# Layer 2 of a four-layer graph network: the boundary between row groups one quad sooner, and products and low parts interleaved

## The reference

```python
h = jnp.maximum(_layernorm(x, axis=-1), 0.0)
x = x + _L2_gnn_ref(h, adj, L2_gnn_W, L2_gnn_a)

def _L2_gnn_ref(x, adj, W, a):
    h = x @ W
    e_src = h @ a[:D, 0]
    e_dst = h @ a[D:, 0]
    e = e_src[:, None] + e_dst[None, :]
    e = jnp.where(e > 0, e, NEG_SLOPE * e)
    att_logits = jnp.where(adj > 0, e, MASK_VAL)
    attention = jax.nn.softmax(att_logits, axis=1)
    h_prime = attention @ h
    return jax.nn.elu(h_prime)
```

## Time and profile before

| | us |
|---|---|
| median of 3 runs | 2366.55 |
| lowest, highest | 2362.13, 2367.09 |
| the profiled execution | 2364.97 |
| its span in the trace | 2363.3 |
| mean granted clock of TensorE | 0.983 |

### The profile page before, as it was taken

How to read it: one execution, slowest core, us unless ns; L and a number is a source line. 1 busy time by engine, 2 the same in 40 slices (tenths; PEclk the granted TensorE clock), 3 DMA queues, 4 the chain that set the end, 5 groups by cost and what they waited for, 6 DMA issues and landing times. The chain is left out here.

```text
span 2363.3 us, 45615 instructions
## 1 busy us (share of the span) xinstructions
PE 2228.8 (94%) x17180; PEld 1702.6 (72%) x17180; DVE 1799.8 (76%) x2845; ACT 1372.6 (58%) x2100; POOL 114.6 (5%) x124
## 2 busy tenths in 40 slices
PE   5799999999999998999978999999999999999998
PEld 4677767778676776888867888878466666666667
DVE  6967788697877856112249999998898898898896
ACT  6555564655656465665655555554465565565656
POOL 2000010010101001000000000000000000000000
PEclk9899999999999999999989999999999999999999
DMA  7542240414321012222211222222211111111000
GB/s 177 112 63 42 58 85 28 81 45 81 51 62 50 28 52 96 81 89 93 80 45 50 71 69 70 67 75 68 84 32 47 31 54 50 36 46 50 23 32 28
DMA packets 62934, 146.72 MB, mean 62 GB/s; under 512 B 10023, under 2 KB 14778, under 8 KB 61757
## 3 DMA queue, kind: packets, MB, share of 16 engines
q1 hardware_dynamic: 56461, 110.57, 15.1%
q0 software_dynamic: 5760, 33.56, 8.6%
q10 hardware_dynamic: 560, 0.52, 0.1%
HBM read 170.30 MB, written 41.43 MB: 90 GB/s over the span
## 5 line engine op out<-in xcount | busy, mean ns | idle before, releaser
L2150 PE MATMUL bank<-VB,arena 128*128 128x257 f16 x1024 | 285.7, 279 | 30.6 <-ACT arena L2036 21.8
L193 PE MATMUL bank<-s_row,kT_hi 128*128 128x512 f16 x1024 | 304.5, 379 | 3.4 <-DVE m_col L2743 1.2
L1559 PE MATMUL bank<-VA,ph 128*128 128x257 f16 x1024 | 281.3, 275 | 6.8 <-DVE VA L1168 6.8
L2153 PE MATMUL bank<-VB,arena 128*128 128x257 f16 x1024 | 284.5, 278 | 0.0
L2151 PE MATMUL bank<-VB,arena 128*128 128x257 f16 x1024 | 284.4, 278 | 0.0
L2857 PE MATMUL bank<-VA,w_dense 128*128 128x257 f16 x1024 | 280.7, 274 | 3.0 <-ACT w_dense L2681 2.4
L1560 PE MATMUL bank<-VA,ph 128*128 128x257 f16 x1024 | 280.9, 274 | 0.0
L1561 PE MATMUL bank<-VA,pl 128*128 128x257 f16 x1024 | 280.8, 274 | 0.0
L2859 PE MATMUL bank<-VA,arena 128*128 128x257 f16 x1024 | 280.2, 274 | 0.0
L2858 PE MATMUL bank<-VA,w_dense 128*128 128x257 f16 x1024 | 280.1, 274 | 0.0
L2015 ACT CAST arena<-arena 128x512 f16<-128x512 f32 x256 | 155.8, 617 | 157.8 <-DVE arena L2067 139.5
(11 more groups left out here) (344 smaller groups left out, 4937.7 us busy)
## 6 DMA issues: line engine op xcount, KB each, us to landing
mask<-mask_d SPq DMA_DIRECT2D x128, 256.0 KB, 2.7
arena<-mask_d SPq DMA_DIRECT2D x128, 256.0 KB, 2.7
mask_d<-in_adj POOLq DMA_DIRECT2D x8, 2048.0 KB, 23.4
xg<-in_x SPq DMA_DIRECT2D x8, 512.0 KB, 11.9
x<-xg SPq DMA_DIRECT2D x8, 512.0 KB, 3.9
xg<-x SPq DMA_DIRECT2D x8, 512.0 KB, 4.2
x<-xo POOLq DMA_DIRECT2D x8, 512.0 KB, 3.0
w_dense<-x SPq DMA_DIRECT2D x8, 512.0 KB, 4.2
```

Source lines behind the costliest of these rows:

```text
L193: last = nc.tensor.matmul(out_ap, st, mv, start=(i == 0), stop=(i == len(todo) - 1))
L1559: nc.tensor.matmul(acc, ph[:, u % HR, c], v_row(V, 0, t), start=(t == 0), stop=False)
L2150: nc.tensor.matmul(acc, p_hi, v_at(V, 0, t), start=first, stop=False)
L2153: last = nc.tensor.matmul(acc, pl[:, slot(q, r), c], v_at(V, 0, t), start=False, stop=final)
```

## The change

Four things. `late` is 0 in layer 2 too, so the reciprocals and scalings stand in part 0 instead of part 1, the fourth reciprocal in quad 1, and the parts with the elu, the moments, the normalisation, the transposes and the split of kT each stand one quad sooner; the queries and values (TensorE's q = 5, the splits' q = 7) stay. Relu and Exp stay in part 1, and so now stand behind the high parts of quad 1, apart from the scalings. Within a quad VectorE takes products and low parts in the order of `ORDER`, with nb ahead of low part 0. After the loop `beside` is called once with -1 ahead of the parts, and its steps are numbered one lower, which leaves that end in its old sequence. The waits that named a product or a low part by number now name it by its place in the new order; they are left out of the diff.

```diff
@@ -1919,7 +1919,7 @@
                 ring = 4 if weighted else 2
-                late = 1 if weighted else 0
+                late = 0 if weighted else 0
                 ph = tile("ph", [P, ring * R, GW], F16)
@@ -1939,7 +1939,8 @@
                 act_q.plan(("hi", R))
-                dve_q.plan(("p32", R), ("lo", R))
+                ORDER = [("p32", 0), ("p32", 1), ("lo", 0), ("p32", 2), ("lo", 1), ("p32", 3), ("lo", 2), ("lo", 3)]
+                dve_q.plan(*((f"{name}{r}", 1) for name, r in ORDER))
                 skip = 0 if weighted else Q - 1
@@ -1970,6 +1971,8 @@
                             part(eng, g - 1, q)
+                    if beside is not None:
+                        beside(-1)
                     for q in range(Q):
...
@@ -2029,7 +2032,7 @@
                     def part(act, g, q):
-                        if q == late:
+                        if q == 0:
                             work["sums_free"](act, g)
@@ -2060,21 +2063,22 @@
                             dve.wait_ge(gam_rowed.sem, gam_rowed.upto(q))
-                        for r in range(R):
-                            dve.wait_ge(dve_q.sem, dve_q.before(n, "lo", r))
-                            if r == 2 and q == 1 + late and not isinstance(g, int):
-                                inverse(g - 1, R - 1, R)
-                            nc.vector.scalar_tensor_tensor(
-                                out=p32[:, r, :], in0=s_row[:, ds(g * GW, GW)],
-                                scalar=omega[:, q * R + r:q * R + r + 1],
-                                in1=mask[:, q % MS, r * GW:(r + 1) * GW], op0=ALU.max, op1=ALU.mult
-                                ).then_inc(dve_q.sem, dve_q.one("p32", r))
-                        if not isinstance(g, int):
-                            middle(g - 1, q)
-                        for r in range(R):
-                            dve.wait_ge(act_q.sem, act_q.at(n, "hi", r))
-                            nc.vector.tensor_tensor(pl[:, slot(q, r), :], p32[:, r, :], ph[:, slot(q, r), :],
-                                                    ALU.subtract).then_inc(dve_q.sem, dve_q.one("lo", r))
+                        for name, r in ORDER:
+                            if name == "p32":
+                                if r == 1 and q == 1 and not isinstance(g, int):
+                                    inverse(g - 1, R - 1, R)
+                                dve.wait_ge(dve_q.sem, dve_q.before(n, f"lo{r}"))
+                                nc.vector.scalar_tensor_tensor(
+                                    out=p32[:, r, :], in0=s_row[:, ds(g * GW, GW)],
+                                    scalar=omega[:, q * R + r:q * R + r + 1],
+                                    in1=mask[:, q % MS, r * GW:(r + 1) * GW], op0=ALU.max, op1=ALU.mult
+                                    ).then_inc(dve_q.sem, dve_q.one(f"p32{r}"))
+                            else:
+                                if r == 0 and not isinstance(g, int):
+                                    middle(g - 1, q)
+                                dve.wait_ge(act_q.sem, act_q.at(n, "hi", r))
+                                nc.vector.tensor_tensor(pl[:, slot(q, r), :], p32[:, r, :], ph[:, slot(q, r), :],
+                                                        ALU.subtract).then_inc(dve_q.sem, dve_q.one(f"lo{r}"))
                         if isinstance(g, int):
@@ -2451,12 +2455,11 @@
                     nc.scalar.activation(e[:, :], ag[:, :], ACT.Relu, scale=-1.0).then_inc(act_s.sem, act_s.one("below"))
-                if q == 1:
                     act.wait_ge(act_s.sem, act_s.at(g, "below"))
                     nc.scalar.activation(e[:, :], e[:, :], ACT.Exp, scale=-1.0).then_inc(act_s.sem, act_s.one("e"))
-                if q == 3:
+                if q == 2:
                     normal(act, g, h, xo, nb, rsx)
-                if q == 5:
+                if q == 4:
                     act.wait_ge(pe_s.sem, pe_s.at(g, "hT", K - 1))
@@ -2467,11 +2470,11 @@
             def dve_middle(dve, g, q):
-                if q == 3:
+                if q == 2:
                     shift(dve, g, nb, mvx, rsx, "nb", "rx")
...
             def dve_part(dve, g, q):
-                if q == 2:
+                if q == 1:
@@ -2681,11 +2684,11 @@
                 def beside(q):
-                    if q == 0:
+                    if q < 0:
                         far_pair(0)
                         far_pair(1)
-                    if 2 <= q <= 5:
-                        far_pair(q)
+                    if 1 <= q <= 4:
+                        far_pair(q + 1)
@@ -2781,17 +2784,17 @@
                 def beside(q):
-                    if q == 0:
+                    if q < 0:
                         own_entries(0)
+                    if q == 1:
+                        add_far(1)
                     if q == 2:
-                        add_far(1)
-                    if q == 3:
                         take_top(1)
...
                         take_top(2)
+                    if q == 3:
+                        add_far(3)
                     if q == 4:
-                        add_far(3)
-                    if q == 5:
                         take_top(3)
```

More of the change, by code:

```diff
@@ L1980, in quad @@
                     def quad(g, q):
-                        eng, stage = (dve_q, "p32") if weighted else (act_q, "hi")
-                        sp.wait_ge(eng.sem, eng.before(g * Q + q, stage, R - 1, MS))
+                        sp.wait_ge(*((dve_q.sem, dve_q.before(g * Q + q, "p323", 0, MS)) if weighted else
+                                     (act_q.sem, act_q.before(g * Q + q, "hi", R - 1, MS))))
                         sp.sem_inc(s_pass[3], 1)
@@ L2011, in quad @@
                             if weighted:
-                                act.wait_ge(dve_q.sem, dve_q.at(g * Q + q, "p32", r))
+                                act.wait_ge(dve_q.sem, dve_q.at(g * Q + q, f"p32{r}"))
                             act.wait_ge(pe_q.sem, pe_q.before(g * Q + q, "pv", r, ring))
@@ L2135, in made @@
                         if weighted:
-                            pe.wait_ge(dve_q.sem, dve_q.at(n, "lo", r))
+                            pe.wait_ge(dve_q.sem, dve_q.at(n, f"lo{r}"))
                             if isinstance(g, int):
@@ L2605, in load_quad @@
                     else:
-                        sp.wait_ge(dve_q.sem, dve_q.at(G * Q - MS + n, "p32", R - 1))
+                        sp.wait_ge(dve_q.sem, dve_q.at(G * Q - MS + n, "p323"))
                     at = (n % slots) * QW
@@ L2621, in load_x @@
                     else:
-                        sp.wait_ge(dve_q.sem, dve_q.at(G * Q - 1, "p32", R - 1))
+                        sp.wait_ge(dve_q.sem, dve_q.at(G * Q - 1, "p323"))
                     sp.wait_ge(s_xout, made_all if g == G - 1 else made_most)
```

## The result

The changed kernel takes 2386.82 us (median of 4 runs, 2385.57 to 2387.72), the one before 2366.27 (4 runs, 2362.13 to 2367.09): a ratio of 1.0093, 95% interval [1.008, 1.0105]. It is slower, by 20.5 us on the medians, where +14 was forecast. The profiled executions took 2386.98 and 2364.97 us.

What follows compares the result with a forecast made beforehand. VectorE and TensorE were taken as nearly equally loaded, VectorE setting the pace after the change. Terms 10.7 + 3.1 + 1 = 14.8 us were taken as +14, giving 2380 us; the forecast's own range was 2372 to 2385.

Steps and rivals of the forecast that it cites:

- Quad 1: Second quad of a group: row scalings ahead of the first high part make VectorE wait 0.93 us.
- group 0: First group, before the loop: late high parts and handover waits in its eight quads add 3.1 us.
- I take a wait of 0.10, with bounds of 0 and 0.35: Quad 2 on VectorE: nb, behind two products instead of four, waits 0.10 us for POOL's root.
- hi to lo 0.63: Each quad: handover from ScalarE's high-part copy to VectorE's low part, start to start, 0.63 us.
- the ruler: Stretch from the loop's start to the last query low part, 365.6 us before; forecast to grow by 10.7 us.
- by the 0.9 us that such a dip costs in a group I add +1: Layer's end: TensorE idles about 6 us, then starts the scores at the lower clock, costing 1 us.
- 14.8, less a rounding for terms that may overlap: Whole kernel: the summed loss of 14.8 us was taken as +14 us, for possibly overlapping terms.
- A: Rival, all quads: skewed order free, the sooner boundary's gain stays, about 2347 us; 0.14 including what lies towards B.
- B: Rival, all quads: shorter handovers, a quad loses 0.2 us; +2, about 2368 us; chance 0.10.
- C: Rival, the groups: TensorE's lower clock costs as well, +19 to +21 us, 2386 us; chance 0.08.
- D: Rival, group boundary: TensorE's wait stays near 2.7 us, VectorE still sets the pace; no time or chance of its own.
- Part one: Group boundary one quad sooner: by itself the period could fall from 52.7 to 50.0 us.

Runs made afterwards that it cites:

- the two experiments with one wait each: Changed kernel with only low part 0's wait left (2361.67 us), or only low part 3's (2366.28 us).
- the boundary alone: Changed kernel with four products and then four low parts in each quad, keeping the boundary one quad sooner: 2354.06 us.
- the skewed order alone: Kernel before with the changed kernel's order in a quad and its own old boundary: 2399.49 us.
- the masks ahead: Changed kernel with SyncE's three mask loads at the layer's end put ahead of the load of the queries: 2379.56 us.
- the first of the two single-wait orders: Changed kernel with products 0 and 1, low part 0, products 2 and 3, then low parts 1 to 3: 2361.67 us.

## Why the prediction was right or wrong

**Right: direction and mechanism.** The order, not the boundary, decides; VectorE sets the pace; a plain quad's two waits stand at low parts 0 and 3 and nowhere else; and the two experiments with one wait each show that they are separate and add up. Quad 1 was forecast at 5.06 + 0.93 = 5.99, without the 0.07 of its reciprocal, and took 1404.14 - 1398.07 = 6.07; quad 3 at 5.06 + 0.78 = 5.84, and took 1420.80 - 1414.94 = 5.86; group 0 at +3.1, and it is 3.46 us longer (58.14 against 54.68), and each of the two lengths comes back within 0.05 us in every kernel of its order. The groups are alike whatever the clock. The first score came 12.9 us behind the query low part by forecast, 13.35 measured.

**Wrong: sizes, all to the same side.** 2386.8 us lies above the forecast's own 2372 to 2385. VectorE's delay at the last query low part was 17.5 us, not 13.8, and own entries started 17.9 later (1672.66 against 1654.75), not 12 to 15. The steps that failed, as terms of the sum:

- "I take a wait of 0.10, with bounds of 0 and 0.35" for nb. Its turn was at 1409.15 + 1.32 = 1410.47, it started at 1410.83: 0.36, the upper bound. POOL's root is at the long end of the earlier trace rows in every group. The row of that line for the stretch 1280 to 1645 alone (ns, min/median/max) said so in the kernel before:

```profile
L1865 POOL TENSOR_TENSOR rstd_x<-ve_x,nhalf x7: 1502/1505/1510, 1302.2 to 1618.4; 128x4 f32<-128x4 f32 x7
```

  I had taken the median of all 16 and not of the seven in the loop. Quad 2 lasted 5.79 instead of 5.46.
- "hi to lo 0.63": 0.65, so 5.50 for a plain quad, not 5.46, 0.2 us a group. kT's low part started 0.44 late instead of 0.32, and the elu's row of VectorE (L2489) shows 0.32 where the forecast had 0.26. With quad 2 this is the period of 54.57 instead of 54.0, and +14.2 on the ruler instead of +10.7.
- "by the 0.9 us that such a dip costs in a group I add +1". The dip in a group was a poor measure: there the granted clock is 0.97 over the whole stretch, here it was 0.50 for all of the first 5 us. It cost +2.5, and another +1.6 at a second place, in layer 3, that the sum had at nothing ("Layer 3 follows unchanged"). The first could have been read ahead: halving the rate of 2.79 us of work costs up to 2.8. The second could not, as far as the runs show.
- "14.8, less a rounding for terms that may overlap": the sum was already too small, and no overlap showed that would have justified the 0.8 us taken off.

In all, 10.7 + 3.1 + 1 = 14.8 were forecast, and 14.2 + 3.3 + 0.4 + 2.5 + 1.6 = 22.0 measured on the spans.

**TensorE's waits.** At the boundary 1.9 us were forecast and 1.76 measured, in quad 2 it is 2.0 and 2.28. The third, 1.4 at quad 5, does not show in that group: no row of TensorE has idle time between 1411.71 and 1447. At a clock of 0.97 TensorE is busy 50.5 us of this group, not the 48.8 that the forecast took. It would cost nothing, since VectorE waits for no row sums in that group.

**The rivals.** A (the skew is free, 2347) is ruled out for this order, and its time is that of its neighbour: the same boundary with three products ahead runs in 2347.75. The agreement is in part luck, since A had a gain of some 2 us at the ends, where that kernel's group 0 is 0.7 us longer than before and its first scores start at the lower clock. The Trainium skill, "VectorE: DVE Perf Modes", section "The DRAIN you can't avoid", is not contradicted: that kernel too has a semaphore on every operation and loses nothing in 5.06 us quads. No run here leaves a semaphore out, so its comparison is not repeated. The section gives no price for a wait on another engine, and that is where the time went. B (half the loss) falls with 5.50 us quads. C has the right time, 2386, by the wrong cause: it put the clock into the groups, where stretches at 0.94 and 0.97 are equally long. The clock's cost, 4.1 us, lies at two places outside them, and the rest of the excess is VectorE's waits. D falls: TensorE's boundary wait did shrink, from 2.72 to 1.76 us. Part one by itself was forecast with a wait of 0.9 us for row sums; the boundary alone shows 1.53, and 50.7 us a group instead of 50.0.

**What stays open.** Why the four scores of layer 3 fell to the lower clock after a wait of 1.17 us that every kernel here has. They did in three of the four kernels with the changed order (the changed one, the skewed order alone, the masks ahead) and in none of the other eight. A slow start of the first scores doesn't decide it: with nb later the first scores were slow and the drop did not come, with the masks ahead it is the other way round. Without the drop the change costs 20.4 us on the spans instead of 22.0. Open too is what moves the kernels ahead of layer 2: VectorE's last step on `omega`, just before its first product there, starts anywhere between 1220.6 and 1223.5 in the twelve kernels, though the edits lie behind it. Group 0 itself does not scatter: it takes 54.7 us with four products ahead (three kernels), 58.1 to 58.2 in the changed order (four) and 55.4 with three products ahead (three).

## What to carry to other kernels

When two engines pass tiles to and fro, measure the round trip start to start (here 0.86 + 0.65 = 1.51 us) and keep at least that much queued work between a tile's departure and its return: two items of 0.66 were 0.19 short, three were enough. With the last item's place, that was 39 us of 2387. Count the last item of a block as well as the first, since it has the least behind it. And where a late chain ends in an idle TensorE, price the work after the idle time at half the clock, from a row at that level.

## What the runs showed of the hardware

- The same twelve score matmuls took 2.79 us after 0.81 us of idle TensorE and 5.32 after 6.63, at granted clocks of 1.00 and 0.50. With 1.44 us (masks ahead) and 2.88 us (boundary alone) of idle time ahead, their first pairs lasted 0.60 and 0.59 us; with 3.65 (three products ahead) the first lasted 0.84 and the next 1.06, with 4.60 (the first of the two single-wait orders) the first lasted 1.01.
- In a timeline grouped by rows a short wait disappears: rows' lengths run on beside the next row's start (0.69 long at a pitch of 0.60), and low part 0, which waited 0.19 us, stands without a bracket. The waits view adds up to 16.2 us for L2080, where turns and starts give some 29: seven groups of 2.2 in the plain quads, 0.93 in quad 1 and 1.04 in quads 2 and 3 (0.24 and 0.80). The prediction looked for some 30 in that view, and 16.2 is what it shows of them.
- POOL's root of 128x4 takes 1.50 to 1.51 us in all seven groups of the loop in layer 2 and 1.01 to 1.04 in the eight of layer 1 (963.0 to 1207.9 in the changed kernel), with the same line and form. The runs don't show why.
